# Second layer's products in column tiles, read out ahead of the second sums; its exponentials ahead of its transposes' copy on ScalarE

## The chip, the core and the metric

The kernel runs on one core of one Trainium2 chip. A core has five engines that run their own instruction lists and meet at semaphores: TensorE (PE; its weight loads are a row of their own, PEld), VectorE (DVE), ScalarE (ACT), GpSimd (POOL) and SyncE (SP), which starts the DMAs. The metric is the time of one execution in microseconds; smaller is better.

## What is computed

`x` is (64, 128, 160): 64 batches of 128 rows with 160 channels. `ctx` is (64, 77, 256). Two layers run one after the other:

```
# layer 0, 20 heads of 64
n = layer_norm(x);   x = x + attention(n, n)       # self: 128 keys
n = layer_norm(x);   x = x + attention(n, ctx)     # cross: 77 keys
n = layer_norm(x);   x = x + geglu_ff(n)
# layer 1, 20 heads of 8, 73 text tokens and 4 image tokens
q = heads(x @ W_q);  k_t, v_t = heads(text @ W_k), heads(text @ W_v)
probs_t  = softmax(q @ k_t.T * scale)
text_out = probs_t @ v_t
qsem     = l2norm(probs_t @ text)                  # 256 wide, one per head and row
fused    = q @ k_ip.T * scale + 0.5 * (qsem @ l2norm(ip).T)
ip_out   = (softmax(fused) * mask) @ v_ip
out      = (text_out + ip_out) @ W_out + b_out + x
```

Layer 1's norm `|probs_t @ text|` is taken as a quadratic form: the probabilities are multiplied by the Gram matrix of the text (73 x 73) and by themselves, and summed.

## The kernel before

**Tiling.** The 64 batches form 16 groups of 4. Time is cut by hand into slots `t`; three slots (parts or subs 0, 1 and 2) make a *beat*, 20 beats make a group. A beat of layer 0 works on one *duo*: two heads for all four batches, beats 0 to 9 of a group on self-attention and 10 to 19 on cross-attention, counted by the duo whose scores are being taken. Layer 1 of a group runs 22 beats later, one step per beat, in the shade of the next group's layer 0: a step is one batch and four heads, so a group has 20 steps. After the last duo some 21 beats have layer 1 alone, the *tail*.

**What sets the order.** Each engine's instruction list is written out by one loop over `t`, with the calls of that slot in a fixed order. No scheduler changes it. An engine waits at an instruction until its semaphores stand, and everything behind that instruction on that engine waits too.

**One beat on PE.** Part 0: `probs_transposed` (16 transposes of the duo's probabilities into PT, both banks), `scores` (the next duo's 16 products of queries and keys into PS, two banks), `probs_v` (the previous duo's 16 products with the values into PV), then projections of queries and keys. Part 1: `probs_transposed1` (4 transposes of a layer 1 step, into PT bank 0), `scores1` (1 product, into PT bank 1), then projections. Part 2: `probs_v1` (8 instructions of 73x128 weights and 86 moving columns, into PV), late jobs, and `wo` (8 products with the output weights).

**Jobs.** Projections, context transposes, the feed-forward and layer 1's small products are "jobs": they take turns in a ring of two PSUM banks, PG. Job n waits until job n-2 has been read out (`read_out`). One kind of job is `xT`: 8 transposes of the layer-normalised rows `nx`, 8 times in a group (beats 2, 5, 7, 8, 12, 14, 17 and 19). ACT copies the result to `nT` (L928), DVE subtracts to get its low parts (L1174 and L1175), and the projections or the feed-forward that follow read it.

**One beat on ACT.** Sub 0: `pt_out` copies the transposed probabilities, `exp` takes the first head's exponentials. Sub 1: a copy of a query job, `ot_out` (PV to OTs), `pt1_out` (L1006, layer 1's transposed probabilities to `PTs1`), the second head's `exp` (L997). Sub 2: `exp1` (L1015, layer 1's exponentials), then the copy to `nT` (L928) if there is an `xT`. In beats 4, 9, 14 and 19 of a group one more exponential (L1072) belongs to the image tokens.

**One beat on DVE.** Sub 0: the maxima of the scores (L1248), and `unit_norms` (L1299, the quadratic form `qq` of step j-2). Sub 1: sums of the first head (L1265), layer 1's maxima (L1257), the copy `sip` (L1260), the sums of the second head. Sub 2: the copy of the values (L1186), the two subtractions for `nT`, and `unit_out` (L1279 to L1291), which reads PV after `probs_v1` and gives it free (`on_done`). GpSimd normalises the probabilities (L1461) and raises `qq` to a power (L1454).

**Waits that matter here.** `exp1` of step j waits for `qq_done` of step j-2, because both use the same half of `SE1`. `probs_v` waits for `on_done`, because `probs_v1` wrote PV. `probs_transposed` waits for `pts1_done`, because layer 1's transposes lie in PT.

## Time and profile before

| | |
|---|---|
| median of 3 runs | 3484.61 us (3483.93 to 3485.42) |
| the profiled execution | 3485.28 us |
| its span in the trace | 3483.4 us |
| PE busy | 3335.4 us, 96% |
| DVE busy | 2438.3 us, 70% |
| ACT busy | 2314.2 us, 66% |
| POOL busy | 1329.5 us, 38% |
| mean granted clock of TensorE | 0.99 |

The profiled execution is within 0.02% of the median. Its span leaves out 1.9 us that lie around it. Busy shares are means over the whole run. In a row of the timeline the first number is the start, the second the length from the first start to the last end of a group of like instructions; matmuls overlap, so the distance from one group's start to the next group's start says what the first one costs PE.

### The profile page before, as it was taken

The numbers are of one execution on the slowest core, as the hardware profiler recorded it, in microseconds if no ns is written. First come the engines' busy times: TensorE is split into PE (matmuls) and PEld (weight loads), VectorE is DVE, ScalarE is ACT, GpSimd is POOL, SyncE is SP. The second block draws the span as 40 slices with busy tenths as digits, with TensorE's granted clock in tenths as the row PEclk, the third lists the DMA queues.
The fourth block names the chain that finished last, engine by engine and source line by source line (L and its number), as shares of the span: only waits on it lengthen the run. The fifth ranks groups of instructions, "written<-read, shape, count | busy, mean of one in ns | idle before, by whom it ended". The sixth has DMA issues, their size and how long they took to land. (4 is left out here: it accounts for less than half of the span.)

```text
span 3483.4 us, 96098 instructions
## 1 busy us (share of the span) xinstructions
PE 3335.4 (96%) x34878; PEld 3131.8 (90%) x34878; DVE 2438.3 (70%) x7677; ACT 2314.2 (66%) x6485; POOL 1329.5 (38%) x1657
## 2 busy tenths in 40 slices
PE   5899999999999999999999999999999999999997
PEld 4789999999899999999999899998999999899987
DVE  6657677767767767677767767767677776777655
ACT  4566676766767676676766767676676766767654
POOL 2223343333434433343433434433343333434333
PEclk9999999999999999999999999999999999999998
DMA  6432324223142332324223142332324223142310
GB/s 157 157 116 69 105 63 126 74 86 103 54 123 70 108 90 68 108 63 122 78 83 105 54 123 68 106 94 63 113 64 118 82 82 106 54 124 68 94 51 11
DMA packets 210732, 313.84 MB, mean 90 GB/s; under 512 B 31232, under 2 KB 167520, under 8 KB 210272
## 3 DMA queue, kind: packets, MB, share of 16 engines
q1 hardware_dynamic: 209984, 307.53, 30.5%
q8 instruction: 290, 4.75, 0.6%
q14 instruction: 170, 1.39, 0.1%
q10 hardware_dynamic: 288, 0.16, 0.0%
HBM read 267.97 MB, written 14.42 MB: 81 GB/s over the span
## 5 line engine op out<-in xcount | busy, mean ns | idle before, releaser
L997 ACT ACTIVATE SE<-PS,mx 128x77 f32<-128x77 f32 (+1 forms) x2560 | 674.8, 355 | 271.9 <-DVE mx L1248 271.2
L1461 POOL TENSOR_TENSOR SE<-SE,rs 128x512 f32<-128x512 f32 (+1 forms) x640 | 552.7, 869 | 625.7 <-DVE rs L1270 625.7
L1454 POOL TENSOR_TENSOR n<-qq,p_half 128x4 f32<-128x4 f32 x320 | 327.4, 1023 | 987.0 <-DVE qq L1299 987.0
L1265 DVE TENSOR_REDUCE sums<-SE 128x4 f32<-128x512 f32 (+1 forms) x640 | 368.3, 576 | 217.8 <-ACT SE L997 217.3
L985 ACT ACTIVATE PTs<-PT 128x1024 f32<-128x1024 f32 (+1 forms) x320 | 326.5, 1020 | 242.3 <-PE PT L811 240.7
L933 ACT ACTIVATE qk<-PG 128x512 f32<-128x512 f32 (+1 forms) x640 | 326.3, 510 | 127.2 <-PE PG L612 125.5
L773 PE MATMUL PW<-w_o,OTs 128*128 128x160 f32 x2560 | 408.8, 303 | 0.0
L1248 DVE TENSOR_REDUCE mx<-PS 128x8 f32<-128x1024 f32 (+1 forms) x320 | 323.0, 1010 | 115.6 <-PE PS L793 113.4
L827 PE MATMUL PV<-PTs,v_sb 128*64 128x128 f32 (+1 forms) x5120 | 351.1, 279 | 12.3 <-DVE SE L1291 12.0
L773 PEld LDWEIGHTS PW<-w_o,OTs 128*128 128x128 f32 x2560 | 359.7, 191 | 0.0
L876 PE MATMUL PV<-later 73*128 73x86 f32 x2560 | 331.0, 272 | 2.3 <-ACT later L1006 1.4
L876 PEld LDWEIGHTS PV<-later 73*128 73x128 f32 x2560 | 315.5, 193 | 4.2 <-ACT later L1006 2.8
L1015 ACT ACTIVATE SE<-PT,mx 128x73 f32<-128x73 f32 x1280 | 310.0, 348 | 12.0 <-DVE sip L1260 11.8
L827 PEld LDWEIGHTS PV<-PTs,v_sb 128*64 128x64 f32 (+1 forms) x5120 | 274.5, 137 | 45.6 <-ACT PTs L985 12.6
L811 PEld LDWEIGHTS PT<-ident,SE 64*128 64x128 f32 (+1 forms) x5120 | 195.6, 142 | 82.6 <-issue 58.6
L811 PE MATMUL PT<-ident,SE 64*128 64x64 f32 (+1 forms) x5120 | 242.2, 233 | 24.5 <-POOL SE L1461 24.4
L635 PE MATMUL PG<-vc_slice,cT 128*77 128x256 f32 x1920 | 255.7, 282 | 6.5 <-DVE vc_slice L1351 4.4
L635 PEld LDWEIGHTS PG<-vc_slice,cT 128*77 128x77 f32 x1920 | 234.5, 147 | 7.6 <-ACT qk L933 5.3
L1006 ACT ACTIVATE later<-PT 73x512 f32<-73x512 f32 x320 | 192.1, 600 | 63.4 <-PE PT L859 63.4
L609 PE MATMUL PG<-nT,q_slice 128*128 128x256 f32 x640 | 217.9, 340 | 15.7 <-DVE w_k_rem L1332 8.8
L1433 POOL TENSOR_SCALAR vp<-mv 128x2 f32<-128x2 f32 x96 | 39.2, 408 | 496.0 <-DVE mv L1115 496.0
L1186 DVE COPY v_sb<-PG 128x512 f32<-128x512 f32 (+1 forms) x320 | 212.1, 663 | 16.5 <-PE PG L635 16.5
(209 smaller groups left out, 8439.1 us busy)
## 6 DMA issues: line engine op xcount, KB each, us to landing
q_slice<-q_split SPq DMA_DIRECT2D x630, 192.0 KB, 2.4
vc_slice<-vc_split SPq DMA_DIRECT2D x155, 512.0 KB, 4.0
kc_slice<-kc_split SPq DMA_DIRECT2D x150, 256.0 KB, 2.9
q1st<-q_hi SPq DMA_DIRECT2D x320, 32.0 KB, 2.1
k1st<-k_hi SPq DMA_DIRECT2D x160, 38.5 KB, 2.2
xres<-in_x_dram SPq DMA_DIRECT2D x32, 160.0 KB, 2.7
q1st<-q_lo SPq DMA_DIRECT2D x160, 32.0 KB, 2.1
out_dram<-x SPq DMA_DIRECT2D x64, 80.0 KB, 1.6
```

The lines of the kernel that those rows point to most:

```text
L635: last = mm(ps, cT[:, g % 2, c, hc, TS * b:TS * b + rows], w[:, c, hw, c0:c0 + n], start=(c == 0 and i == 0), stop=(c == 1 and i == 2))
L773: last = mm(PW[:, C * b:C * b + C], OTs[:, n % 2, 128 * b:128 * b + 128], w_o[n // U0][:, p, :], start=(p == 0 and b == 0), stop=(p == NP ...
L811: last = tr(PT[0:J, r, at:at + 64], SE[rows, n % 4, J * i:J * i + J], ident[rows, rows])
L827: last = mm(PV[DH * e:DH * e + DH, HT * u + 128 * b:HT * u + 128 * b + 128], v_sb[0:J, d % 2, b, 2 * u + e, :], PTs[0:J, q % 2, u, at:at + ...
L876: last = mm(PV[:, GV * i + off:GV * i + off + GS + D1], PTs1[0:TT, 128 * i:128 * i + 128], gv[:, b % 2, 2 * w + i // 2, off:off + GS + D1] ...
L933: a_(qk[:, i % 2, 0:w, :].rearrange("p a n -> p (a n)"), ps[:, 0:w * HT], ACT.Copy)\
L985: a_(PTs[0:J, q % 2, :, :].rearrange("p u (i r k) -> p r (u i) k", r=2, k=64), PT[0:J, :, :].rearrange("p r (x k) -> p r x k", k=64), ACT. ...
L997: last = a_(SE[:, n % 4, J * i:J * i + J], PS[:, e, J * at:J * at + J], ACT.Exp, bias=mx[:, q % 2, 4 * e + at:4 * e + at + 1])
L1248: v.tensor_reduce(mx[:, q % 2, :].rearrange("p (e x) -> p e x", e=2), PS[:, :, 0:4 * J].rearrange("p e (x j) -> p e x j", j=J), AX, ALU.ma ...
L1265: v.tensor_reduce(sums[:, n % 2, :], SE[:, n % 4, 0:4 * J].rearrange("p (i j) -> p i j", j=J), AX, ALU.add)\
L1454: gp.tensor_tensor(n20[:, b % 2, 4 * w:4 * w + 4], qq[:, b % 2, 4 * w:4 * w + 4], p_half[:, 0:4], ALU.pow)\
L1461: gp.tensor_tensor(e, e, rs[:, n % 2, :].unsqueeze(2).to_broadcast([128, 4, J]), ALU.mult)\
```

## The change

On PE, `probs_v1` cuts its weights into two column tiles of 64: 16 instructions with 64 weight columns instead of 8 with 128. Both tiles see the same 86 moving columns and write the upper and the lower 64 partitions of the same result. The result goes to PT bank 0 instead of PV. The function moves from part 2 of the beat after its step to part 0 of the second beat after it, behind `probs_v`. `probs_transposed1` moves behind the jobs of part 1 and writes PV instead of PT bank 0. Each of the two takes over the waits of its new bank.

`xT` leaves the jobs: a function of its own, `norm_transposed`, writes it to PS bank 0, waits for the exponentials of the duo that has its scores there, and tells `xT_full`. `scores`, next to write PS, waits for `nT_dve`, the end of the two subtractions on DVE.

On ACT, `pt1_out` moves from ahead of the second exponentials to behind `exp1`, ahead of the `nT` copy. On DVE, `unit_out` moves from sub 2 to sub 1, ahead of the second head's sums, one beat later; `unit_norms` from sub 0 to behind those sums. GpSimd's `norms_of` moves from sub 0 to sub 1. In the tail layer 1's scores use PS bank 1 in every other step, and wait for the exponentials of two steps before.

```diff
         def tail_slot(g, b):
-            return 3 * l1_beat(g, W1 * b + W1 - 1) + 7
+            return 3 * l1_beat(g, W1 * b + W1 - 1) + 8
...
+        def scores1_bank(g, k):
+            return PS[:, 1, :] if alone(g, k) and k % 2 else PT[:, 1, :]
...
+                def norm_transposed(name, scored):
+
+                    pe.wait_ge(S["nx_done"], NORM[name[1:]] + 1)
+                    if scored:
+                        pe.wait_ge(S["exp_done"], 2 * scored)
...
+                            last = tr(PS[:, 0, HT * part + 128 * b:HT * part + 128 * b + 128],
+                                      nx[:, b, 128 * part:128 * part + 128], ident[:, :])
+                    last.then_inc(S["xT_full"], 1)
+                    turned_x[0] = NORM[name[1:]] + 1
...
                     if q > 0:
                         pe.wait_ge(S["exp_done"], 2 * q)
+                    if turned_x[0]:
+                        pe.wait_ge(S["nT_dve"], turned_x[0])
                     for n in (2 * d, 2 * d + 1):
...
-                    if turned1[0]:
-                        pe.wait_ge(S["pts1_done"], turned1[0])
+                    if product1[0]:
+                        pe.wait_ge(S["on_done"], product1[0])
...
-                    if product1[0]:
-                        pe.wait_ge(S["on_done"], product1[0])
+                    if turned1[0]:
+                        pe.wait_ge(S["pts1_done"], turned1[0])
...
-                        last = mm(PV[:, GV * i + off:GV * i + off + GS + D1], PTs1[0:TT, 128 * i:128 * i + 128],
-                                  gv[:, b % 2, 2 * w + i // 2, off:off + GS + D1], start=True, stop=True)
+                        for c in range(2):
+                            last = mm(PT[64 * c:64 * c + 64, 0, GV * i + off:GV * i + off + GS + D1],
+                                      PTs1[0:TT, 128 * i + 64 * c:128 * i + 64 * c + 64],
+                                      gv[:, b % 2, 2 * w + i // 2, off:off + GS + D1], start=True, stop=True)
...
-                    if sub == 1 and l1_at(beat - 1):
-                        pt1_out(*l1_at(beat - 1))
...
                     if sub == 2 and l1_at(beat):
                         exp1(*l1_at(beat))
+                    if sub == 2 and l1_at(beat - 1):
+                        pt1_out(*l1_at(beat - 1))
```

**PE, part 0 and part 2 of one beat.** First the piece that starts at `scores`, before and after; then the piece behind the projection of the values (L617 to L620 before, L623 to L626 after).

```order
L793 MATMUL PS<-qk 128x128 [waits qk_done,exp_done]
L793 MATMUL PS<-qk 128x128 x3
L793 MATMUL PS<-qk 128x128 [waits qk_done]
L793 MATMUL PS<-qk 128x128 x3
L827 MATMUL PV<-PTs,v_sb 64x128 [waits ots_done,on_done,v_done,pts_done]
L827 MATMUL PV<-PTs,v_sb 64x128 x7
L609 MATMUL PG<-nT,q_slice 128x256 [waits q_in0,qk_done]
```

In the changed kernel the same stretch of PE reads:

```order
L809 MATMUL PS<-qk 128x128 [waits qk_done,nT_dve,exp_done]
L809 MATMUL PS<-qk 128x128 x3
L809 MATMUL PS<-qk 128x128 [waits qk_done]
L809 MATMUL PS<-qk 128x128 x3
L843 MATMUL PV<-PTs,v_sb 64x128 [waits ots_done,pts1_done,v_done,pts_done]
L843 MATMUL PV<-PTs,v_sb 64x128 x7
L896 MATMUL PT<-later 64x86 [waits on_done,pts_done,pts1_done]
L896 MATMUL PT<-later 64x86 x7
L615 MATMUL PG<-nT,q_slice 128x256 [waits q_in0,qk_done]
```

Layer 1's products have come in behind `probs_v`, in column tiles, and `scores` has `nT_dve` among its waits. Part 2 of the beat before, ahead of and behind the norm transposes (`xT`, out of `nx`), was this:

```order
L876 MATMUL PV<-later 128x86 [waits on_done,ots_done,pts1_done]
L876 MATMUL PV<-later 128x86 x3
L677 MATMUL PG<-ident,nx 128x128 [waits nx_done,qk_done]
L677 MATMUL PG<-ident,nx 128x128 x3
L773 MATMUL PW<-w_o,OTs 128x160 [waits ots_done]
```

and is now this:

```order
L878 MATMUL PV<-ident,SE 73x128 [waits pts1_done,ots_done,exp1_done]
L878 MATMUL PV<-ident,SE 73x128 x3
L771 MATMUL PS<-ident,nx 128x128 [waits nT_dve,exp_done,nx_done]
L771 MATMUL PS<-ident,nx 128x128 x3
L787 MATMUL PW<-w_o,OTs 128x160 [waits ots_done]
```

Layer 1's transposes stand where its products stood, and the norm transposes have left the PG ring.

**ACT, the last two subs of a beat with an `xT`.** `later` is PTs1. L978 is `ot_out`, L1027 the squares of the context, which only some beats have, L1015 is `exp1`. Before:

```order
L933 ACTIVATE qk<-PG 128x512 [waits job_full]
L978 ACTIVATE OTs<-PV 128x512 [waits wo_done,pv_done]
L1006 ACTIVATE later<-PT 73x512 [waits pv1_done,pt1_done]
L997 ACTIVATE SE<-PS,mx 128x128 [waits pt_done,mx_done]
L997 ACTIVATE SE<-PS,mx 128x128 x3
L933 ACTIVATE qk<-PG 128x512 [waits job_full]
L1027 ACTIVATE kx,cst<-shared 82x256 [waits c_sq,c_dve,c_in]
L1027 ACTIVATE kx,cst<-shared 82x256 [waits c_sq]
L1015 ACTIVATE SE<-PT,mx 128x73 [waits qq_done,sip_in,mx1_done]
L1015 ACTIVATE SE<-PT,mx 128x73 x3
L928 ACTIVATE nT<-PG 128x512 [waits job_full]
```

After the change the same eleven rows stand in this order:

```order
L957 ACTIVATE qk<-PG 128x512 [waits job_full]
L1002 ACTIVATE OTs<-PV 128x512 [waits wo_done,pv_done]
L1021 ACTIVATE SE<-PS,mx 128x128 [waits pt_done,mx_done]
L1021 ACTIVATE SE<-PS,mx 128x128 x3
L957 ACTIVATE qk<-PG 128x512 [waits job_full]
L1051 ACTIVATE kx,cst<-shared 82x256 [waits c_sq,c_dve,c_in]
L1051 ACTIVATE kx,cst<-shared 82x256 [waits c_sq]
L1039 ACTIVATE SE<-PT,mx 128x73 [waits qq_done,sip_in,mx1_done]
L1039 ACTIVATE SE<-PT,mx 128x73 x3
L1030 ACTIVATE later<-PV 73x512 [waits pv1_done,pt1_done]
L952 ACTIVATE nT<-PS 128x512 [waits xT_full]
```

The copy to PTs1 went from the third place to the tenth, directly ahead of the copy to `nT`.

**DVE, from layer 1's maxima of a beat with an `xT` to the maxima of the next beat.** Before:

```order
L1257 TENSOR_REDUCE mx<-PT 128x4 [waits s1_done]
L1260 COPY sip<-PT 128x16 [waits job_full]
L1265 TENSOR_REDUCE sums<-SE 128x4 [waits exp_done]
L1270 RECIPROCAL rs<-sums 128x4 [waits p_done,sum_done]
L1186 COPY v_sb<-PG 128x512 [waits job_full]
L1174 TENSOR_TENSOR nT<-PG,nT 128x256 [waits nT_act,job_full]
L1175 TENSOR_TENSOR nT<-PG,nT 64x256
L1279 RECIPROCAL rr<-PV 128x4 [waits pv1_done]
...
L1291 TENSOR_TENSOR SE<-PV,SE 128x292
L1248 TENSOR_REDUCE mx<-PS 128x8 [waits s_done]
L1299 TENSOR_REDUCE qq<-SE 128x4 [waits on_done]
```

and after:

```order
L1284 TENSOR_REDUCE mx<-PT 128x4 [waits s1_done]
L1287 COPY sip<-PT 128x16 [waits job_full]
L1307 RECIPROCAL rr<-PT 128x4 [waits pv1_done]
...
L1319 TENSOR_TENSOR SE<-PT,SE 128x292
L1292 TENSOR_REDUCE sums<-SE 128x4 [waits exp_done]
L1297 RECIPROCAL rs<-sums 128x4 [waits p_done,sum_done]
L1327 TENSOR_REDUCE qq<-SE 128x4 [waits on_done]
L1213 COPY v_sb<-PG 128x512 [waits job_full]
L1201 TENSOR_TENSOR nT<-PS,nT 128x256 [waits nT_act,xT_full]
L1202 TENSOR_TENSOR nT<-PS,nT 64x256
L1275 TENSOR_REDUCE mx<-PS 128x8 [waits s_done]
```

`unit_out` (five rows, of which two are shown) now precedes the second sums, and `qq` stands behind them, ahead of the copy of the values and of `nT`.

## Rows read from the trace of the kernel before

**Rows 1.** The page's first part: busy us, share, instructions.
```profile
PE 3335.4 (96%) x34878; PEld 3131.8 (90%) x34878; DVE 2438.3 (70%) x7677; ACT 2314.2 (66%) x6485; POOL 1329.5 (38%) x1657
```

**Rows 2.** Waits of PE: what waited, for whom, total us, times, longest.
```profile
PE PV L827 <- DVE SE L1291: 12.0, 15, 1.7
...
PE PG L677 <- ACT qk L933: 4.4, 15, 0.8
```

**Rows 3.** Timeline of PE: start, length, line, tiles, count.
```profile
1490.95 1.02 PE L876 MATMUL PV<-later 73*128 73x86 f32 x8
1491.81 1.29 PE L773 MATMUL PW<-w_o,OTs 128*128 128x160 f32 x8
...
1495.67 1.09 PE L827 MATMUL PV<-PTs,v_sb 128*64 128x128 f32 x16
1496.70 0.39 PE L609 MATMUL PG<-nT,q_slice 128*128 128x256 f32 x1
```

**Rows 4.** Windows of L827: length; PE, PEld busy (instructions); clock; DMA.
```profile
1505.40:1505.52 0.12, 0.09 (x2) 0.09 (x4) 1.00 0.08 17
...
1505.40:1506.18 0.78, 0.75 (x14) 0.75 (x16) 1.00 0.21 55
```

**Rows 5.** Timeline of PE in beat 2 of a group.
```profile
1719.31 1.02 PE L876 MATMUL PV<-later 73*128 73x86 f32 x8
...
1722.72 1.11 PE L793 MATMUL PS<-qk 64*128 64x128 f32 x16
```

**Rows 6.** Timeline of ACT in the same beat.
```profile
1718.12 0.61 ACT L1006 ACTIVATE later<-PT 73x512 f32<-73x512 f32 x1
1718.59 1.15 ACT L997 ACTIVATE SE<-PS,mx 128x128 f32<-128x128 f32 x4
...
1721.07 0.92 ACT L1015 ACTIVATE SE<-PT,mx 128x73 f32<-128x73 f32 x4
1721.88 0.59 ACT L928 ACTIVATE nT<-PG 128x512 fp32r<-128x512 f32 x1
```

**Rows 7.** Timeline of DVE in the same beat; brackets: idle before, releaser.
```profile
1718.60 0.16 DVE L1260 COPY sip<-PT 128x16 f32<-128x16 f32 x1
1719.78 0.69 DVE L1265 TENSOR_REDUCE sums<-SE 128x4 f32<-128x512 f32 x1 [1.01 <-ACT SE L997]
...
1720.59 0.66 DVE L1186 COPY v_sb<-PG 128x512 f32<-128x512 f32 x1
1722.58 0.42 DVE L1174 TENSOR_TENSOR nT<-PG,nT 128x256 fp32r<-128x256 f32 x1 [1.33 <-ACT nT L928]
...
1723.48 0.18 DVE L1279 RECIPROCAL rr<-PV 128x4 f32<-128x4 f32 x1
...
1724.32 1.21 DVE L1248 TENSOR_REDUCE mx<-PS 128x8 f32<-128x1024 f32 x1
```

**Rows 8.** Timeline of DVE in beat 14, cross-attention.
```profile
1844.19 0.16 DVE L1260 COPY sip<-PT 128x16 f32<-128x16 f32 x1
1844.61 0.47 DVE L1265 TENSOR_REDUCE sums<-SE 128x4 f32<-128x308 f32 x1 [0.26 <-ACT SE L997]
1845.12 0.18 DVE L1270 RECIPROCAL rs<-sums 128x4 f32<-128x4 f32 x1
```

**Rows 9.** Timeline of PE, the scores behind that beat.
```profile
1847.73 1.07 PE L793 MATMUL PS<-kx,qk 64*128 64x77 f32 x16
```

**Rows 10.** L859 in the tail: ns min/median/max, first and last start, form.
```profile
L859 PE MATMUL PT<-ident,SE x64: 272/273/421, 3411.0 to 3468.1; 128*73 128x128 f32 x64
```

**Rows 11.** Timeline of DVE in the tail.
```profile
3428.51 0.46 DVE L1299 TENSOR_REDUCE qq<-SE 128x4 f32<-128x292 f32 x1
3429.45 0.46 DVE L1257 TENSOR_REDUCE mx<-PT 128x4 f32<-128x292 f32 x1 [0.48 <-PE PT L845]
```

**Rows 12.** Timeline of ACT in the tail.
```profile
3430.07 1.05 ACT L1015 ACTIVATE SE<-PT,mx 128x73 f32<-128x73 f32 x4 [0.17 <-DVE sip L1260]
```

**Rows 13.** All engines in a stretch of the tail; clock 0.86.
```profile
3375.00:3483.00 108.00, 84.76 (x596) 76.66 (x594) 65.37 (x279) 49.97 (x144) 39.29 (x47) 0.86 0.06 16
```

More of the change, by code:

```diff
@@ L407, in jobs_at @@
                 first, v = first[:1], v + first[1:]
-            return first + v, [x for x in late_at(t) if x[0] != "v"]
+            return first + v, [x for x in late_at(t) if x[0] not in ("v", "xT")]
         JOBS = [j for t in range(FIRST, LAST) for j in jobs_at(t)[0] + jobs_at(t)[1]]
@@ L890, in _ @@
                             probs_v(*duo_at(beat - 1))
-                    if part == 1 and l1_at(beat - 1):
-                        probs_transposed1(*l1_at(beat - 1), turned)
+                        if l1_at(beat - 2):
+                            probs_v1(*l1_at(beat - 2), turned)
                     if part == 1 and l1_at(beat):
@@ L1005, in pt1_out @@
                         act.wait_ge(S["pv1_done"], j - 1)
-                    a_(PTs1[0:TT, :], PT[0:TT, 0, :], ACT.Copy).then_inc(S["pts1_done"], 1)
+                    a_(PTs1[0:TT, :], PV[0:TT, :], ACT.Copy).then_inc(S["pts1_done"], 1)
                 def exp1(g, k):
@@ L1371, in _ @@
                         softmax_in(*duo_at(beat + 1))
-                    if sub == 0 and l1_at(beat - 2):
-                        unit_norms(*l1_at(beat - 2))
                     for g, h in preps_at(t - 2):
@@ L1392, in _ @@
                             job(name)
+                    if sub == 1 and l1_at(beat - 2):
+                        unit_out(*l1_at(beat - 2))
                     if sub == 1 and duo_at(beat + 1):
@@ L1395, in _ @@
                         prob_sums(g, 2 * d + 1)
+                    if sub == 1 and l1_at(beat - 2):
+                        unit_norms(*l1_at(beat - 2))
                     for name in late_at(t):
@@ L1401, in _ @@
                             job(name)
-                    if sub == 2 and l1_at(beat - 1):
-                        unit_out(*l1_at(beat - 1))
                     if sub == 2 and duo_at(beat - 1):
```

66 lines of the change are left out of this document (38 added, 28 removed).

## The prediction

> **What bounds the kernel now.** I read the page's busy shares first. PE is busy for 96% of the span, DVE and ACT for 70% and 66% [rows 1]. So time goes where PE's work goes, and any new idle time of PE is added whole. Second, the list of what PE waits for: it is short, and of it the change touches two entries, `probs_v` behind `unit_out` (12.0 us in all) and `xT` behind ACT's copy of a query job (4.4 us) [rows 2]. Third, the timeline of PE, ACT and DVE through one beat with an `xT` [rows 5 to 7], since there the change puts a new wait in front of PE. Last, the tail [rows 10 to 13], where PE isn't the bound.
>
> A difference of 0.2% is 7 us, about what a measurement of this kernel can tell from none. The sum is made against the profiled execution, 3485.3 us, which stands 0.7 us above the median.
>
> **The column tiles.** From the start of L876 to the next group's start pass 0.86 us for 8 instructions, 0.107 each; they move only 86 columns, and `wo` behind them moves 160 [rows 3]. The price of L876 is therefore that of its weights, 128 columns each. L827 is the row nearest to the new form: 16 instructions in two column tiles of 64, 1.03 us from start to start with 128 moving columns [rows 3]. Its windows show how: 2 matmuls had been counted after 0.12 us, 14 after 0.78, so 6 pairs took 0.66 us, 0.11 a pair, with the loads beside them [rows 4]. If the moving columns are what counts in a pair, 86 of them take 0.11 x 86/128 = 0.074, and 8 pairs 0.59 us: 0.27 less than now. Some 300 of the 320 steps lie where PE is the bound: **-81 us**. The bounds: 0.51 a group if one of the 8 pairs hides in its neighbours, 0.35 less than now, -105 us; and the whole 1.03 of L827, +0.17 each, +51 us. I take 0.59: L827 is the nearest row, and its pairs ran at one steady rate, which its columns explain better than a fixed cost.
>
> The rows show that in L827 the load of one pair doesn't add to the stream of the one before: half of L876's 0.107 for half the weight columns is 0.054, and 0.054 + 0.11 would be 0.16 a pair, where 0.11 is read [rows 3, 4]. The Trainium skill says otherwise ("TensorE: Matmul & The Clock Gate", Part 3, The mechanism): a weight load overlaps with running matmuls only when the row group differs, and column tiles share theirs. By that rule a new pair would take 0.054 + 0.074 = 0.128, the group 1.02 us, and this term would be +48 us and not -81. The trace of L827 speaks against it. What that costs otherwise is the third rival.
>
> **Waits that go.** `probs_v` no longer waits for `unit_out`, which is a beat old by then, and `xT` no longer for the PG ring: 12.0 + 4.4 [rows 2], **-16 us**.
>
> **What the new wait of `scores` costs.** `xT` now lies in PS bank 0, so the next `scores` waits for the last subtraction on DVE. Before, only projections a full part later needed `nT`. Beat 2 shows how late that is. PE began `scores` at 1722.72 [rows 5]; DVE ended the subtractions only as L1279 began, 1723.48 [rows 7]. So even with nothing moved, `scores` would have started 0.8 us late. Now the moves. `unit_out` takes 0.84 (L1279 at 1723.48 to L1248 at 1724.32) and starts behind `sip`: 1718.68 + 0.84 = 1719.52 [rows 7]. The second exponentials ran from 1718.59 [rows 6]. They win the 0.48 of the copy to PTs1 (L1006 to L997 [rows 6]), and lose the 0.59 by which layer 1's products, now in part 0, delay the query job that ACT copies ahead of them: they end 0.1 later, and the second sums start at 1719.90 and take 0.81 (L1265 to L1186 [rows 7]), to 1720.71. `qq` takes 0.46 [rows 11], to 1721.17. `exp1` waits for it, and begins at 1721.27 with 0.1 for the hop (L1015 began at 1721.07 before). It takes 0.81 until the next instruction (L1015 to L928 [rows 6]), to 1722.08. There the copy to PTs1 comes in, 0.48, to 1722.56, and the `nT` copy needs 0.70 until L1174 starts (1721.88 to 1722.58 [rows 6, 7]): 1723.26. The subtractions need 0.90 (L1174 to L1279 [rows 7]), 1724.16, and 0.11 to PE: `scores` start at 1724.27. Without the wait they would start at 1722.72 - 0.27 = 1722.45. PE stands idle for **1.8 us**. Nothing is queued on PE that could fill it; `probs_v`, layer 1's products and every projection stand behind `scores`.
>
> In beat 14, with cross-attention, `sip` ends at 1844.27, `unit_out` at 1845.11, the sums 0.60 later (1844.61 to 1845.12, and the reciprocal's 0.09 [rows 8]), `qq` at 1846.17, `exp1` starts at 1846.27, the copy at 1847.08, 0.48 for it and some 0.2 for the image tokens' exponential, 1847.8 for `nT`, and 1.7 to `scores`: 1849.5. Unstalled: 1847.73 - 0.27 = 1847.46 [rows 9]. That is 2.0; 1.8 is taken, since a part of the early delay is PE's own and moves both. The same steps at the other six places of a group give 1.7 (beat 5, where the feed-forward in the same beat reads `nT` and waits), 0 (beat 7, whose next `scores` come 3.5 us later than the chain), 1.7 (beat 8), 1.1 (12), 1.3 (17) and 2.3 (19). The sum is 11.7 us a group. Layer 1 runs beside 15 of the 16 groups: **+175 us**. The bounds: 6 a group, if `exp1` isn't held by `qq`, +90; and 15, if each place costs what beat 14 costs, +225.
>
> **What DVE's new order costs elsewhere.** The copy of the values (L1186) frees a bank of PG. It now stands behind `unit_out` and `qq`, 0.84 + 0.46 = 1.3 us later in its list, less what DVE had idle (1.01 ahead of the second sums [rows 7]). In beats 1, 6 and 9 of a group a job two places on waits for that bank: 0.4 each, estimated from that difference of 0.3 and the hop, some 1.25 a group, **+19 us**; from 0 to 60.
>
> **The tail.** There a step took (3468.1 - 3411.0)/17, 3.36 us [rows 10], on a chain through three engines. The new order makes one ring of all: layer 1's products 0.59 and hop 0.11, its scores 0.4, the maxima and `sip` 0.55 (L1257 at 3429.45, `exp1` at 3430.07 [rows 11, 12]), `unit_out` 0.8, `qq` 0.46 [rows 11], hop 0.1, `exp1` 0.81, copy 0.6, hop 0.1: 4.5 us. That is 1.15 a step for some 17 steps, **+20 us**. The alternate bank gives none of it back, since the ring doesn't pass through that wait. From -10 to +25.
>
> **Sum.** -81 - 16 + 175 + 19 + 20 = +117: 3602.3 against the profiled execution's 3485.3, and with the 0.7 between that and the median 3602.
>
> **Rivals.**
>
> *The chain to `nT` is hidden* (faster). If the engines ahead of `nT` run ahead of PE by about 2 us in the changed kernel, the wait of `scores` ends before PE arrives; then -97 remains of the terms above, with the ring and the tail at nothing: 3388. The point from which it decides is 97 us in all for the waits at `xT` and the others, 6.5 a group. For it speaks that DVE and ACT have 30% idle [rows 1]. Against it, that the chain starts from PE's own scores of the same beat, so they can't run ahead of it, and that 0.8 us of lateness stood there before any move. 0.12.
>
> *`qq` doesn't bind, only ACT's order does.* Then beats 14 and 17 stall little, 6 us a group in all: -97 + 90 + 39 = +32, 3517. For it: in beat 2 `exp1` moves by only 0.2. Against it: in beat 14 it moves by 1.4. 0.10.
>
> *Column tiles don't pay.* Pairs at 0.107 to 0.128: 0.86 to 1.02 us a group, so 81 to 129 us more than forecast, 3683 to 3731. For it: no row has 86 moving columns in column tiles. 0.08.
>
> *The clock.* The granted clock was 0.86 in the tail, where PE was busy for 84.76 of 108 us [rows 13], and 1.00 in the windows of L827 [rows 4]. The new idle time would take PE from 96% to 93% in the mean, but a beat with a 1.8 us hole in some 10.5 is 83% busy. If the clock fell to 0.86 for a tenth of the whole, 14% of some 300 us more, it would be +40: 3642. 0.07.
>
> **How the numbers follow.** The forecast has 0.58, with 3555 to 3655 as its own range from the bounds of its terms. The case between it and the first rival, in which the waits come to just about 6.5 us a group, has 0.05. The others have 0.12, 0.10, 0.08 and 0.07. The range takes in the second rival (3517), the clock (3642) and the third from its near end (3683) to its middle: 3510 to 3700. Out fall the first rival, the case between and the third's far end, 0.19. Faster by over 0.2% is the first rival, 0.12; within is the case between, 0.05; slower is the rest, 0.83.
>
> **What would show it.** L896 takes 0.59 us from start to start. In the list of PE's waits `scores` (L809) waits for DVE's L1202 some 90 to 105 times, 150 us together, and the feed-forward's L615 for the rest. On ACT `exp1` (L1039) waits for DVE's `qq` (L1327) in most beats. The cycle of the tail is 4.5 us. I am wrong if L809 waits less than 60 us in all, or if L896 takes over 0.8.

## The result, and the profile after

The change made the kernel slower: 3736.59 us median of 4 runs (3732.85 to 3737.33) against 3484.42 us, a ratio of 1.072 with a 95% interval of 1.070 to 1.074. The forecast was 3602 us with a range of 3510 to 3700. The sign was right. The loss is 252 us, twice the 117 that were forecast, and the time lies above the range.

The page of the changed kernel begins like this (span, then busy us, share and instructions of each engine):

```profile
span 3733.9 us, 101387 instructions
## 1 busy us (share of the span) xinstructions
PE 3369.2 (90%) x37438; PEld 3156.6 (85%) x37438; DVE 2398.8 (64%) x7677; ACT 2340.7 (63%) x6485; POOL 1323.5 (35%) x1657
```

PE was at 96% [rows 1] and is at 90%. It is even busy for 34 us more, though its work got smaller: that is the first hint at the clock, whose mean fell from 0.990 to 0.963. What PE waits for (what waited, for whom, total us, times, longest):

```profile
PE PS L809 <- issue: 90.5, 74, 1.7
PE PG L615 <- DVE nT L1202: 64.6, 32, 2.6
PE PT L827 <- issue: 42.8, 47, 1.4
PE PT L896 <- ACT later L1030: 28.2, 17, 3.0
PE PG L738 <- DVE later L1219: 21.7, 16, 3.7
PE PG L615 <- DVE kx L1209: 17.0, 30, 0.7
...
PE PG L733 <- DVE later L1219: 10.5, 16, 1.1
```

L809 is `scores`, L615 the feed-forward or a projection, L827 `probs_transposed`, L896 layer 1's products. "issue" means that the profile names no releaser; who it is shows in the timeline below. On ACT the wait that the forecast named is there, the one of `exp1` (L1039) for `qq` (L1327):

```profile
ACT SE L1039 <- DVE qq L1327: 326.4, 287, 4.5
```

Set side by side beat for beat, from one `scores` to the next, the median over the groups 2 to 14 says where the time went: beat 0 +2.85 us, beat 19 +2.70, 5 +2.55, 8 +1.47, 2 +1.41, 14 +1.29, 6 +1.16, 17 +1.00, 12 +0.90, 9 +0.57, 10 +0.49. Beats in which nothing waits (11, 13, 15, 16) give 0.1 to 0.25 back, and beat 3, where `probs_v` no longer waits for `unit_out`, 0.57. From the first `scores` to the last it is 220 us, and the tail has 30.

**The column tiles.** PE behind `scores`, in the changed kernel (start, length, line, tiles, count):

```profile
1116.13 1.09 PE L843 MATMUL PV<-PTs,v_sb 77*64 77x128 f32 x16
1117.05 0.77 PE L896 MATMUL PT<-later 73*64 73x86 f32 x16
1117.75 0.38 PE L615 MATMUL PG<-nT,q_slice 128*128 128x256 f32 x1
```

From L843 to L615 pass 1.62 us, where from L827 to L609 it was 1.03 [rows 3]: the new group adds 0.59 to 0.60, as forecast, for the 0.86 that L876 took. From its own start to the next group's start it is 0.70; the value products ahead of it take 0.92 where they took 1.03.

**The chain to `nT` in beat 2.** ACT, DVE and PE of the changed kernel, one fence each:

```profile
1156.33 0.95 ACT L1039 ACTIVATE SE<-PT,mx 128x73 f32<-128x73 f32 x4
1157.16 0.60 ACT L1030 ACTIVATE later<-PV 73x512 f32<-73x512 f32 x1
1157.64 0.60 ACT L952 ACTIVATE nT<-PS 128x512 fp32r<-128x512 f32 x1
```

```profile
1155.79 0.43 DVE L1327 TENSOR_REDUCE qq<-SE 128x4 f32<-128x292 f32 x1
...
1158.34 0.42 DVE L1201 TENSOR_TENSOR nT<-PS,nT 128x256 fp32r<-128x256 f32 x1 [1.53 <-ACT nT L952]
1158.78 0.43 DVE L1202 TENSOR_TENSOR nT<-PS,nT 64x256 fp32r<-64x256 f32 x1
```

```profile
1157.39 0.71 PE L827 MATMUL PT<-ident,SE 64*128 64x64 f32 x16 [0.37 <-issue]
1159.31 0.94 PE L809 MATMUL PS<-qk 64*128 64x128 f32 x12 [1.21 <-issue]
```

`exp1` starts 0.11 behind `qq`'s end, but its row has no bracket: ACT wasn't idle, it came straight from the squares of the context, which some beats have ahead of `exp1`. So in beat 2 ACT's own list is as late as `qq`. The copy to PTs1 starts 0.83 later, the copy to `nT` 0.48 later, the subtraction 0.70 later, `scores` 0.97 later, at 1159.31. The links have the lengths of [rows 6, 7]. The second brackets are what the wait cost: 1.21, and 0.37 ahead of the transposes, together 1.6 where 1.8 was forecast. In beat 4, below, ACT stood idle for `qq`.

**What the 0.37 is.** In beat 4 there is no `xT`, and still PE stands for 1.43 us ahead of its transposes. ACT, then PE:

```profile
1176.42 0.96 ACT L1039 ACTIVATE SE<-PT,mx 128x73 f32<-128x73 f32 x4 [1.30 <-DVE qq L1327]
```

```profile
1177.48 0.71 PE L827 MATMUL PT<-ident,SE 64*128 64x64 f32 x16 [1.43 <-issue]
```

`exp1` ends at 1177.38, and the transposes begin 0.1 later. They wait for `exp1_done`, because layer 1's scores lie in bank 1 of PT. That wait stood in the code before; there these transposes waited for GpSimd's probabilities instead, twice 0.45 us in beat 4. PE in the kernel before:

```profile
1740.95 0.46 PE L811 MATMUL PT<-ident,SE 64*128 64x64 f32 x8 [0.46 <-POOL SE L1461]
1741.86 0.46 PE L811 MATMUL PT<-ident,SE 64*128 64x64 f32 x8 [0.44 <-POOL SE L1461]
```

The forecast overlooked the wait for `exp1`.

**The clock.** PE in beat 0 of group 5 and of group 9 (window; length; PE busy with instructions; granted clock; DMA share and GB/s):

```profile
1129.89:1138.94 9.05, 9.05 (x110) 1.00 0.34 96
2018.24:2030.37 12.13, 12.13 (x110) 0.72 0.27 77
```

The same 110 instructions take 9.05 us at a clock of 1.00 and 12.13 at 0.72. Between the two levels of 2.4 and 1.2 GHz, 0.72 means that PE ran at 1.2 for a bit over half of the window, 6.8 us, which cost 3.1. Ahead of it PE had stood for 2.7 us at the end of beat 19, in two pieces: 1.06 ahead of the transposes and 1.67 ahead of `scores`. The clock fell in beat 0 of all groups from 2 on but two (5 and 6), and in many also in beat 5, where PE waits 2.5 us for `nT`, and in beat 7. Beat 5 in the groups 5 and 9:

```profile
1177.99:1192.51 14.52, 11.88 (x138) 1.00 0.11 30
2069.39:2084.91 15.52, 13.07 (x138) 0.89 0.09 26
```

Group 5, the only one of the groups 2 to 14 with full clock in all beats, loses 10.2 us against before; the others lose 11 to 17.

### The profile page after: what moved, and what is told of

Its sections match the earlier page's. It is cut to its first block, busy times and chain, and to the rows that moved or that the text cites. A ratio compares the mean times of both kernels' runs of the same rounds, so it can differ in the third digit from the quotient of the medians.

```text
span 3733.9 us, 101387 instructions
## 1 busy us (share of the span) xinstructions
PE 3369.2 (90%) x37438; PEld 3156.6 (85%) x37438; DVE 2398.8 (64%) x7677; ACT 2340.7 (63%) x6485; POOL 1323.5 (35%) x1657
## 4 chain that ended last, share of the span: by engine, by line
PE 71%; DVE 11%; ACT 9%; issue 7%; POOL 0%; DMA 0%; SPq 0%; ACTq 0%; DVEq 0%; POOLq 0%
PE PV L843 9%; PE PS L809 9%; PE PT L827 6%; PE PG L615 6%; PE PW L787 6%; PE PG L641 5%; PE PT L896 5%; PE PG L632 3%; PE PG L618 3%; PE PG L617 3%; PE PG L616 3%; ACT SE L1021 3%; PE PG L717 2%; DVE sums L1292 2%; PE PV L878 2%
## 5 line engine op out<-in xcount | busy, mean ns | idle before, releaser
L1039 ACT ACTIVATE SE<-PT,mx 128x73 f32<-128x73 f32 x1240 | 296.1, 322 | 294.1 <-DVE qq L1327 294.1
L843 PE MATMUL PV<-PTs,v_sb 128*64 128x128 f32 (+1 forms) x5120 | 367.1, 288 | 2.7 <-ACT later L1030 2.7
L843 PEld LDWEIGHTS PV<-PTs,v_sb 128*64 128x64 f32 (+1 forms) x5120 | 286.8, 142 | 36.2 <-issue 6.2
L827 PEld LDWEIGHTS PT<-ident,SE 64*128 64x128 f32 (+1 forms) x5120 | 197.5, 143 | 113.8 <-issue 100.6
L827 PE MATMUL PT<-ident,SE 64*128 64x64 f32 (+1 forms) x5120 | 241.0, 233 | 56.3 <-issue 42.8
L896 PE MATMUL PT<-later 73*64 73x86 f32 x5120 | 259.7, 245 | 28.4 <-ACT later L1030 28.2
L896 PEld LDWEIGHTS PT<-later 73*64 73x64 f32 x5120 | 236.1, 142 | 34.8 <-ACT later L1030 33.3
L615 PE MATMUL PG<-nT,q_slice 128*128 128x256 f32 x640 | 223.6, 349 | 29.5 <-DVE kx L1209 17.0
L809 PE MATMUL PS<-qk 64*128 64x128 f32 x2560 | 194.0, 294 | 41.8 <-issue 41.8
L1499 POOL TENSOR_TENSOR kbd<-k1st,head_of_row 96x308 fp32r<-96x308 f32 x320 | 223.4, 698 | 0.0
```

Source lines behind the costliest of these rows:

```text
L615: mm(ps, w[0][:, c0:c0 + 128], nT[:, b, 0, :], start=True, stop=False)
L809: last = mm(PS[:, e, at:at + J], qk[rows, n % 2, 0, 128 * b:128 * b + 128], keys[rows, J * b:J * b + J], start=True, stop=True)
L827: last = tr(PT[0:J, r, at:at + 64], SE[rows, n % 4, J * i:J * i + J], ident[rows, rows])
L843: last = mm(PV[DH * e:DH * e + DH, HT * u + 128 * b:HT * u + 128 * b + 128], v_sb[0:J, d % 2, b, 2 * u + e, :], PTs[0:J, q % 2, u, at:at + ...
L896: last = mm(PT[64 * c:64 * c + 64, 0, GV * i + off:GV * i + off + GS + D1], PTs1[0:TT, 128 * i + 64 * c:128 * i + 64 * c + 64], gv[:, b % ...
```

## The experiments

Each is compared with the kernel before, which ran on the same chip. The beat figures are medians over groups 2 to 14.

### Column tiles alone

```diff
-                        last = mm(PV[:, GV * i + off:...], PTs1[0:TT, 128 * i:128 * i + 128], ...)
+                        for c in range(2):
+                            last = mm(PV[64 * c:64 * c + 64, GV * i + off:...],
+                                      PTs1[0:TT, 128 * i + 64 * c:128 * i + 64 * c + 64], ...)
```

> The kernel before with one edit: layer 1's products in two column tiles of 64, at their old place in part 2 and still in PV. Theory (the tile term is real, 0.26 us less a step, as the changed kernel's trace has it: 0.60 where 0.86 stood): 300 x 0.26 = 78 us less, about 3407 us, granted clock 0.99 as before. Rival (column tiles pay only behind other column tiles, here they stand between ordinary projections and the output weights; and they lower the clock): less than 40 us gained, 3445 to 3485, or the clock lower than 0.99.

Measured: 3491.24 us, ratio 1.0017 (1.0006 to 1.0029), clock 0.991. The rival is right that nothing is gained, but not by the clock. PE of this kernel:

```profile
1491.38 0.28 PE L620 MATMUL PG<-w_v_rem,nT 128*128 128x256 f32 x1
1491.59 0.82 PE L877 MATMUL PV<-later 73*64 73x86 f32 x16
1492.34 0.95 PE L773 MATMUL PW<-w_o,OTs 128*128 128x160 f32 x5
```

The group takes 0.75 and not 0.59, and the step into it 0.21, where a projection before costs 0.12. And the load rows (PEld) show that the first load of the group starts with the first matmul, where before it ran during the last projection. This kernel, then the kernel before, whose L876 began at 1490.95 [rows 3]:

```profile
1491.59 0.64 PEld L877 LDWEIGHTS PV<-later 73*64 73x64 f32 x16
```

```profile
1490.83 0.98 PEld L876 LDWEIGHTS PV<-later 73*128 73x128 f32 x8
```

Between full tiles and column tiles there is a seam with no overlap. The step out costs too: the output weights now take 1.08 to the next group where they took 1.01. So 0.11 is saved in the group, and 0.09 and 0.07 are lost at its two ends. Behind `probs_v`, itself in column tiles, the products share that group's two seams, and there the gain is seen.

### The changed kernel without column tiles

```diff
-                        for c in range(2):
-                            last = mm(PT[64 * c:64 * c + 64, 0, ...], PTs1[0:TT, 128 * i + 64 * c:...], ...)
+                        last = mm(PT[:, 0, ...], PTs1[0:TT, 128 * i:128 * i + 128], ...)
```

> The changed kernel with one edit undone: layer 1's products in 8 instructions of 128 weight columns again, at the new place in PT bank 0. Theory: 0.26 us more a step where PE isn't waiting, less where the wait for nT swallows it (the chain to nT doesn't start later with it in most places): 3737 + 50 to 80 = 3787 to 3817, waits of PE as in the changed kernel, clock within 0.01 of 0.963. Rival (the column tiles lower the clock): clock back at 0.98 or more and the time below 3737.

Measured: 3865.02 us, ratio 1.109 (1.105 to 1.114), clock 0.950. That is 128 us more, above the expected 50 to 80: the waits are the same (`scores` 90.5 us), so they swallow next to nothing; only the one in beat 4 shrinks, by 0.3. PE of this kernel:

```profile
1197.32 1.10 PE L843 MATMUL PV<-PTs,v_sb 128*64 128x128 f32 x16
1198.35 1.12 PE L895 MATMUL PT<-later 73*128 73x86 f32 x8
1199.26 0.36 PE L615 MATMUL PG<-nT,q_slice 128*128 128x256 f32 x1
```

1.94 us from L843 to L615 against 1.62, 0.32 a step and 96 in all. The rest goes with the clock, which fell from 0.963 to 0.950: here it also falls in beat 13 of most groups, behind the same wait of 1.0 us in beat 12. Beat 13 of group 8, in the changed kernel and in this one:

```profile
1941.03:1949.16 8.13, 8.13 (x102) 1.00 0.39 115
```

```profile
1999.33:2009.20 9.87, 9.87 (x93) 0.83 0.30 100
```

The column tiles are not what lowers the clock.

### The transposes of the norm in the ring again

```diff
+                    elif kind == "xT":
...
-                    if turned_x[0]:
-                        pe.wait_ge(S["nT_dve"], turned_x[0])
...
-                            norm_transposed(name, min(max(beat + 2, 0), DUOS * GROUPS))
+                            job(name)
```

> The changed kernel with one edit undone: the transposes of the normalised rows are jobs in the PG ring again, and the scores no longer wait for the subtractions on VectorE. Theory (the wait of the scores for nT is the main loss): the waits of the scores at beats 2, 8, 12, 14 and 19 (6.2 us a group in the changed kernel's trace) go, and with them most of the clock's falls behind beat 19; the feed-forward's wait in beats 5 and 17 (4.1 us a group) stays, since nT is as late there: 3737 - 15 x 6.2 - 30 to 60 = 3585 to 3615. Rival (the ring takes over the wait: the transposes wait for a bank, or the next job waits for nT as the reader of the ring): less than 50 us gained, over 3687.

Measured: 3671.95 us, ratio 1.054 (1.051 to 1.057), clock 0.978. 65 us are gone, between theory and rival, and both are in the trace. Beats 2 and 14 lose their stall whole (+1.41 to +0.02, +1.29 to -0.19), beat 0's fall of the clock is gone (those in the beats 5 and 7 stay in about half of the groups). But beat 8 gets no better (+1.79), and the ring waits: the transposes for the copy of the values 36 us in all, the "down" job for `nT` 26. The wait of `scores` for `nT` is one of several ways in which a late `exp1` reaches PE.

### Filling the idle time

```diff
+                def fill(n):
+                    for _ in range(n):
+                        mm(PS[:, 1, 0:C], ident[:, :], w_o[0][:, 0, :], start=True, stop=True)
+
+                FILL_S = {2: 8, 8: 7, 12: 7, 14: 9, 19: 11}
...
+                    fill(FILL_S.get((q - 2) % DUOS, 0) if g and q > DUOS + 2 else 0)
```

> The changed kernel with added work alone: products of the unit matrix with output weights, thrown away in PS bank 1, put where PE waits (7 to 16 of them ahead of the scores behind beats 2, 8, 12, 14 and 19, ahead of the transposes behind beat 19, and ahead of the feed-forward in beats 5 and 17), each group a little shorter than the wait it fills. Theory (the idle time of PE makes the granted clock fall, and that costs some 5 us a group): clock back at 0.98 to 0.99, time 3737 - 60 to 85 = 3652 to 3677. Rival (the waits are the whole cost, the clock follows from something else): clock at 0.96 and the time at 3737 or above.

Measured: 3833.60 us, ratio 1.100 (1.097 to 1.103), clock 0.982. The clock came back, and in beat 0 all of its time (+2.85 to -0.22). But the fill was sized by taking the 0.13 us of an instruction of L773 [rows 3] for that of a product, and a product of these is two instructions in the trace (22 for 11 products here), some 0.29 us. So the fill outlasted the waits: beat 19 went from +2.70 to +4.96. This run tells of the clock, but not of its price. So it was made shorter:

> The changed kernel with the same added and thrown-away products as in the run with the long fill, but about half as many (3 to 7 a place): there each had taken 0.30 us and not 0.13, so the fill outlasted the waits, and the scores started later than nT was there. Theory (idle time of PE costs clock, some 5 us a group): the waits stay as long as in the changed kernel, filled in part or whole, beat 0 takes 9.1 us in all groups and not 12.1, the clock is 0.98, and the time 3737 - 50 to 75 = 3662 to 3687. Rival (the fall of the clock is not caused by these waits): beat 0 at 12.1 in most groups, 3730 or more.

Measured: 3674.68 us, ratio 1.055 (1.052 to 1.058), clock 0.983. Beat 0 in the groups 5 and 9 of this run:

```profile
1109.63:1118.69 9.06, 9.06 (x110) 1.00 0.34 99
1990.24:1999.30 9.06, 9.06 (x111) 1.00 0.37 101
```

Beats 2, 8, 12, 14 and 19 are as long as in the changed kernel to within 0.1 us (19: +2.66, 2: +1.41). What got shorter are the beats in which the clock had fallen: 0 by 3.1, 5 by 1.0 and 7 by 1.5 in the median. Only work that is thrown away was added, and the kernel got 62 us faster. So the falls of the clock behind the stalls cost about these 62 us. A few are left: from the first `scores` to the last the clock's records give 211 us at the lower level in the changed kernel, 53 in this one, and 33 before the change. At the rate at which 158 of them cost 62, the 20 that are left make some 8 us more, an estimate.

### ScalarE's order

```diff
+                    for name in late_at(t):
+                        if name[0] == "xT":
+                            job(name)
                     if sub == 2 and l1_at(beat - 1):
                         pt1_out(*l1_at(beat - 1))
...
-                        job(name)
+                        if name[0] != "xT":
+                            job(name)
```

> The changed kernel with one order undone: on ScalarE the copy to nT goes ahead of the copy to PTs1. Theory (ScalarE's order is one link of the chain to the scores): nT comes 0.6 us earlier at each of the 7 places, 15 x 7 x 0.5 to 0.6 = 52 to 63 less, and some clock back where a wait gets short: 3737 - 55 to 90 = 3647 to 3682. Rival (the copy to PTs1, now later, holds up layer 1's products or the next copy of the probabilities, as PE waits for it in the scores' place): less than 25 us gained.

Measured: 3649.38 us, ratio 1.047 (1.044 to 1.051), clock 0.972: 87 us less, as the theory has it. Beats 2, 8, 12, 14, 17 each get 0.46 to 0.62 shorter, beats 5 and 19 0.9 to 1.5, and beat 7, in which the clock fell, 1.4.

### A third buffer for `exp1`

```diff
-        SE1 = sb("SE1", [128, 2, 512])
+        SE1 = sb("SE1", [128, 3, 4 * 80])
...
-                    if j > 2:
-                        act.wait_ge(S["qq_done"], j - 2)
+                    if j > 3:
+                        act.wait_ge(S["qq_done"], j - 3)
```

> The changed kernel with a third buffer for layer 1's exponentials, so that exp1 of step j waits for the quadratic form of step j-3 and no longer of step j-2, which VectorE now makes only just before. Theory (this wait holds the chain at beats 8, 12, 14, 17 and 19, not at beat 2, where the squares of the context stand ahead of exp1): stalls at beats 12, 14 and 17 shrink by 0.8 to 1.2 each, at 2 by 0.1, and a tail step gets 0.4 to 0.5 shorter: 15 x 3.5 = 52 and 8 from the tail, 3737 - 60 to 90 = 3647 to 3677. Rival (the wait of exp1 costs nothing, since ScalarE's own order or VectorE's sums come as late): within 15 us of 3737.

Measured: 3598.53 us, ratio 1.033 (1.029 to 1.037), clock 0.973. 138 us less, more than the 60 to 90 expected, and more than any other single edit. Of the three beats that the theory gives 0.8 to 1.2, 12 and 14 give less (0.6 and 0.4), 17 gives 1.05. The surplus is elsewhere: beat 4, which has no `xT`, goes from -0.17 to -0.93, beats 5, 6 and 8 lose 2.1, 0.9 and 1.0, and the tail some 17 where 8 were expected. The fall of the clock in beat 0 isn't gone: it gets longer, and beat 0 goes from +2.85 to +3.96; beat 19, ahead of it, still has 2.6 us of waits. In its list of PE's waits the transposes are held by GpSimd, as before the change, and no longer by `exp1`:

```profile
PE PT L827 <- POOL SE L1489: 20.6, 39, 4.5
```

Of the links cut one at a time, the wait for `qq` gives the most back.

### The quadratic form last on VectorE

```diff
-                    if sub == 1 and l1_at(beat - 2):
-                        unit_norms(*l1_at(beat - 2))
                     for name in late_at(t):
                         if name[0] == "v":
                             job(name)
...
+                    if sub == 2 and l1_at(beat - 2):
+                        unit_norms(*l1_at(beat - 2))
```

> The run with the third buffer, and the quadratic form moved on VectorE from ahead of the copy of the values and the subtractions to behind them. Theory (VectorE's list is late by that 0.46 us for the jobs that wait for a bank of the ring): of the waits at beats 5, 6, 8, 9, 18 of a group some 0.4 each go, 15 x 2 = 30 us less than the run with the third buffer alone. Rival (the quadratic form costs these jobs nothing, VectorE waits there anyway): within 8 us of that run.

Measured: 3558.51 us, ratio 1.021 (1.018 to 1.024), 40 us less than with the third buffer alone, where the theory has 30. But of the beats that it names only 9 gains 0.35. Beats 1, 3 and 10 get 0.3 to 0.4 shorter, and in 1 and 3 the wait for the copy of the values is what went; the other half is in the chain to `nT`, 0.8 in beat 19 and 0.4 in beat 14, whose subtractions now come ahead of the quadratic form. So the sum is partly luck.

### The four edits together, and the tail

> The changed kernel with four of its links cut together: three buffers for layer 1's exponentials, the quadratic form behind the subtractions on VectorE, the copy to nT ahead of the copy to PTs1 on ScalarE, and the transposes of the normalised rows back in the PG ring, so that the scores don't wait for nT. The column tiles behind the value products stay. Theory (the chain to nT is what cost, and the column tiles are worth 0.17 to 0.25 us a beat where nothing waits): beats 2, 12, 14 and 19 give 1.3, 0.5, 0.75 and 1.6 us against the run with the quadratic form last, beats 5 and 8 some 0.7, no falls of the clock behind beat 19; a group comes out 3 to 4 us shorter than before the change: 3485 - 15 x 3.5 + 18 for the tail = 3450, from 3435 to 3475. Rival (the ring takes the waits over, as at beats 0 and 8 of the run with the ring alone): 3485 to 3520.

Measured: 3502.10 us, ratio 1.0054 (1.0037 to 1.0072), clock 0.986. Behind the first groups one fall of the clock is left, in one beat. A group is 0.1 to 0.2 us shorter than before the change, not 3 to 4. Against the run with the quadratic form last 56 us are gained, where the theory had 108. Beats 2, 14 and 19 gave what it says, within 0.15; beats 8 and 12 got 0.95 and 0.26 longer, and the rival names why. PE's waits in this kernel:

```profile
PE PG L683 <- DVE v_sb L1215: 25.0, 31, 1.0
...
PE PG L764 <- DVE v_sb L1215: 10.1, 14, 0.7
```

L683 is the transposes of the norm, waiting for a bank that the copy of the values frees. The tail is at 156 us, 18 over that of before. The next run puts the copy to PTs1 ahead of `exp1` in the tail:

> The combined kernel, and in the tail the copy to PTs1 ahead of exp1 on ScalarE, where before it stood behind. Theory (in the tail exp1, the copy to PTs1, the products and the next scores are one ring): a step gets shorter by the copy, 0.5 to 0.6 us, 17 x 0.55 = 9 us less than the combined kernel. Rival (the ring of the tail goes by another way, through the wait of the transposes for exp1 or through VectorE): within 3 us of it, or slower.

Measured: 3502.61 us, ratio 1.0061 (1.0046 to 1.0076): nothing. The rival was right that the ring goes another way, though by neither of the two that it names. PE of this kernel in the tail:

```profile
3462.74 0.82 PE L900 MATMUL PT<-later 73*64 73x86 f32 x16 [0.57 <-DVE SE L1323]
3464.98 0.38 PE L868 MATMUL PT<-kbd,q1st 96*128 96x308 f32 x1 [1.43 <-POOL kbd L1503]
```

and GpSimd at the same time:

```profile
3463.16 1.01 POOL L1486 TENSOR_TENSOR n<-qq,p_half 128x4 f32<-128x4 f32 x1 [4.55 <-DVE qq L1331]
3464.14 0.70 POOL L1503 TENSOR_TENSOR kbd<-k1st,head_of_row 96x308 fp32r<-96x308 f32 x1
```

The block of keys for the next scores stands on GpSimd behind the power of `qq`, 1.01 us, and that waits for a late `qq`. So:

```diff
-                    if sub == 2 and l1_at(beat + 1):
-                        own_keys(*l1_at(beat + 1))
...
+                    if sub == 1 and l1_at(beat + 1):
+                        own_keys(*l1_at(beat + 1))
                     if sub == 1 and l1_at(beat - 2):
                         norms_of(*l1_at(beat - 2))
```

> The kernel with the tail's copy first, and on GpSimd the next step's block of keys (kbd) made ahead of the power of the quadratic form, not behind it. Theory (the tail's ring goes through GpSimd: the quadratic form, its power 1.0 us, the keys 0.7, then layer 1's scores, which waited 1.43 us for the keys in the tail's trace): the tail falls from 156 us to 140 to 145, where it was 138 before the change; 3502 - 11 to 16 = 3486 to 3491. Rival (the tail is held by PE's clock or by ScalarE): less than 4 us gained.

Measured: 3481.30 us, ratio 0.9997 (0.9988 to 1.0006). The tail is 141 us, 17 less; in all it is 21 less, where 11 to 16 were expected.

### The copy of the values first, everywhere and at three beats

> The kernel with the keys first, and on VectorE the copy of the values ahead of layer 1's reading out and not behind it; the second sums are ahead of both. Theory (the reading out, 0.84 us, now stands ahead of the copy that frees a bank of the ring: waits for it at beats 3, 8, 12 and 19 are 2.8 us a group in the combined kernel's trace, and that for the keys in beat 8, 0.7, is another's): 15 x 2 to 2.8 = 30 to 42 less than the run with the keys first, 3445 to 3460, which would be 1% faster than before the change. Rival (the reading out, now at the end of the beat, holds the next beat's transposes of the probabilities, which wait for bank 0 of PT): at or above the run with the keys first.

Measured: 3478.98 us, ratio 0.9989 (0.9980 to 0.9998), 2 us less and not 30 to 42. Beats 8 and 12 get 0.84 and 0.76 shorter, but beats 0, 2, 4, 5 and 7 each 0.1 to 0.6 longer: there PE's transposes wait for the reading out, 16.9 us in beat 4 alone over the run, where about half of that was a wait for GpSimd in the run with the keys first. The rival's wait was right and nearly as big as the gain. The next run makes the exchange only where it pays:

```diff
+                    values_first = beat % DUOS in (8, 12, 19)
-                    if sub == 1 and l1_at(beat - 2):
+                    if sub == 1 and l1_at(beat - 2) and not values_first:
                         unit_out(*l1_at(beat - 2))
...
+                    if sub == 1 and l1_at(beat - 2) and values_first:
+                        unit_out(*l1_at(beat - 2))
```

> The kernel with the keys first, and VectorE's copy of the values ahead of the reading out only in beats 8, 12 and 19 of a group. Theory (at these three the copy of the values is what a job waits for, at the others the reading out is what the next transposes wait for): beats 8, 12 and 19 come out as in the run with the values first everywhere (0.84, 0.76 and 0.26 us shorter), beats 0, 2, 4, 5 and 7 as in the run with the keys first: 15 x 1.6 to 1.9 = 24 to 28 less than that run, 3453 to 3458, 0.8% faster than before the change. Rival (the wait moves on to the next place, as it did between those two runs): over 3472.

Measured: **3450.62 us**, ratio 0.990 (0.989 to 0.992): 1% faster than the kernel before, and 286 us less than the changed kernel. A group is 2.2 us shorter than before. The page of this kernel:

```profile
span 3448.4 us, 101227 instructions
## 1 busy us (share of the span) xinstructions
PE 3267.4 (95%) x37438; PEld 3057.5 (89%) x37438; DVE 2405.0 (70%) x7677; ACT 2338.0 (68%) x6485; POOL 1325.9 (38%) x1657
```

PE is busy for 68 us less than before [rows 1]. And the same kernel with 128 weight columns:

> The same kernel with layer 1's products in 8 instructions of 128 weight columns, no column tiles. Theory (column tiles behind column tiles are worth 0.31 us a step: 0.70 to the next group where 0.91 stood, and 0.92 for the value products where 1.02 stood): 300 x 0.25 to 0.31 = 75 to 93 more than with them, 3530 to 3550. Rival (PE has slack at many beats, so the tile term is only partly there): less than 60 more.

Measured: 3533.15 us, ratio 1.0146 (1.0129 to 1.0164), 82.5 us more. This is the tile term nearly alone: from the first `scores` to the last, where 77 of the 82.5 lie, both kernels have the same time at the lower clock, and PE's waits differ only in beat 4, by 0.3 us. It shows one thing more. This kernel has all the repairs and no column tiles, and is 1.4% slower than the kernel before: the new order, even so repaired, costs 49 us by itself, and what gains is the tiles.

## Why the prediction was wrong, step by step

The step that failed most is the one that left the granted clock out of the sum: it is set beside the stalls as a rival, and the runs show it as a consequence of them, at 62 us or a little more. Next come the waits for the ring (19 forecast, 46 measured), the tail (20 and 30), and a wait of `probs_transposed` that the sum lacks (11).

**The column tiles: -81 forecast.** Right: the group adds 0.60 for 0.86, and the pair of the last two runs gives 82.5 us. That price holds for the new place, where full tiles cost 0.91 and not 0.86. By the rule of the Trainium skill ("TensorE: Matmul & The Clock Gate", Part 3, The mechanism) the forecast's estimate for a group was 1.02 us. The trace of L896 says 0.60 to 0.70, so the measurement decides against the rule here. What the forecast did not see is that the gain belongs to the place: between full tiles it is nothing.

**The waits that go: -16.** They went: neither is in the list of after.

**The stalls at `xT`: +175.** The mechanism and nearly the size were right. PE's waits in the timeline make 1.6 us at beat 2, 1.9 more than before at 5, none at 7, 1.0 at 8, 1.0 at 12, 1.3 at 14, 1.2 more at 17 and 2.7 at 19: 10.7 a group for 11.7 forecast, 161 us. Each stood where the text put it, though beats 8 and 14 have less than forecast and 19 has more. The sign that was named didn't come out so well: `scores` waits 90.5 us in 74 waits, where 150 in 90 to 105 were forecast. The rest stands at the feed-forward, and ahead of `probs_transposed` in the beats 2 and 19.

**VectorE's order elsewhere: +19.** Mis-sized. The waits for the ring (for `later`, `kx` and `v_sb`, with the smaller rows of the list) are 64 us, where they were 18: +46. The forecast took the copy of the values to be late by 0.3 us and counted three places; the feed-forward's and the context's copies stand behind it in the same list. The runs with the quadratic form last and with the values first show a part of the size. The biggest of these waits, 1.1 us in beat 6 for the feed-forward's copy, is not of that list: with the third buffer it falls to 0.2, so it is the late `exp1` again.

**A wait that the sum lacks.** The step "nothing is queued on PE that could fill it" looked only at what stands behind `scores`. `probs_transposed`, ahead of it, waits for `exp1`, and `exp1` for `qq`. Ahead of it PE waits 1.42 us in beat 4, where it waited 0.90 for GpSimd before, and 0.22 in beat 10: 0.74 a group more, 11 us. With the third buffer the wait in beat 4 is 0.4.

**The tail: +20.** It was 30. The steps that the forecast priced take 5.3 us in the mean and not 4.5, at a granted clock of 0.79 in the tail where it was 0.87. Before, they took 3.8 and not 3.36: the 64 instructions of [rows 10] are 16 steps, so the 57.1 us are to be divided by 15. With 3.8 the forecast would have been 11 us for this term, a third of what came. And the kernels from the combined one on show that a part of the ring goes through GpSimd, which the forecast did not have.

**The clock.** This is the step that failed most. The forecast has it as a rival with a chance of 0.07, beside the stalls, as if one or the other would come. But the falls stand behind the stalls in all but one of the groups 2 to 14, and filling the stalls gave 62 us back. So a term for it should have stood in the sum, where it is at nothing. Its price as a rival was 40. With 62 in the sum the forecast would have been 3664, still 73 below the measured time.

The sum as measured is -81 - 16 + 161 + 46 + 11 + 30 + 62 = 213 of 252 us. 18 more are there if a quiet beat gives 0.2 instead of 0.26 us, which the beats 13, 15 and 16 show, though not why. Some 21 us stay open. The falls that the shorter fill left would be 8 of them, by the estimate above; the rest is spread over beats with several waits, which no run took apart.

**The rivals.** That the chain to `nT` is hidden is refuted by the 90.5 us that `scores` waited. That `qq` doesn't bind is refuted by the third buffer. That column tiles don't pay is refuted by the last pair of runs. That the clock falls was right, and came together with the forecast's own case.

## What to carry to other kernels

Where an engine's order is moved, list every consumer of the last thing that gets late, those that stand ahead of the place too: here the exponentials of layer 1, late because VectorE now makes `qq` just ahead of them, reached PE through `scores`, `probs_transposed`, the feed-forward and the ring, and cutting one way left waits at the others. Where a change brings stalls, put a term for the clock into the sum, and not beside it. A change can hold a real gain of 2.4% and lose 7%: the gain came out in the kernel that had a third buffer, new orders on three engines and `xT` back in the ring. Which of these it needed, no run shows one by one.

## What the hardware showed

- Column tiles between full tiles gained nothing: 0.75 us for the group where full tiles took 0.86, 0.09 more for the step into it and 0.07 for the step out. Behind another column-tiled group they added 0.60 in all, where full tiles in that place added 0.91.
- A product of these 32-bit tiles is two matmul instructions in the trace (22 for 11 in the long fill). The counts of products of `wo`, `scores`, `probs_v` and `probs_v1` told ahead of the prediction (8, 16, 16, 8) are counts of these instructions, two to a product, and an `xT` is 4 transposes. No term of the sum rests on the difference, since all were priced from start to start; the long fill did, and missed.
- Stalls of 2.7 us in one beat, none longer than 1.7, brought the granted clock down in the next one, mostly for 6.8 us, in most groups and not in all. Thrown-away products in the same place kept it at 1.00 and made the kernel 62 us faster.
- The length of a stall didn't decide it alone: behind the same wait of 1.0 us in beat 12 the clock fell in beat 13 in 10 of the groups 2 to 14 without column tiles, and in none of them with.
